# A first route over thirteen batches instead of twelve, one step later, with its stores in pairs

## The chip, the cores and the metric

The kernel runs on one core of a Trainium2 chip. The metric is the device time of one execution in microseconds (us). Before the change three runs gave 716.4, 717.88 and 718.25 us; their median, 717.88, is the time that the change is compared with.

## What is computed

A two-layer block on `x` of 16 batches with 128 rows of width 128, with a context `ctx` of 77 rows a batch. All in float32. Cut to what matters:

```python
x = x + tanh(g_xattn[0]) * xattn0(ctx_1024, layernorm(x), mask, ...)   # 16 heads of 64, keys from ctx and x
x = x + tanh(g_ffn[0])   * ffn0(layernorm(x), ...)                     # 128 -> 512 -> 128, gelu
x = x + tanh(g_xattn[1]) * xattn1(layernorm(x), ctx_1024, ...)         # 16 heads of 8, top 32 of 77 scores
x = x + tanh(g_ffn[1])   * moe(layernorm(x), Wr, br, W1, W2)

def moe(x):                                  # rows = 16 * 128 = 2048, 8 experts of 128 -> 512 -> 128
    route = sigmoid(x @ Wr + br)
    e = argmax(route, axis=1)                # one expert a row
    return max(route) * (gelu(x @ W1[e]) @ W2[e])
```

The change touches only the last line: how rows are sorted by expert before the expert products.

## The kernel before, in words

**Steps and slots.** The sixteen batches go through a software pipeline, written out by hand for each engine in its own program. In step i, batch i is prepared, batch i-1 (`A`) does the first attention, i-2 (`A2`) its end and the first feed-forward net, i-3 (`B`) and i-4 (`C`) the second attention, and i-5 (`E`) its output, the layer norm of the router (`r_z`) and the router's logits. A step has eight slots, and the steps run from 0 to 20. Step 18 still has B = 15, C = 14, E = 13; step 19 has C = 15, E = 14; step 20 has E = 15 alone. VectorE (DVE) finds the top 32 of 77 scores in rounds of MAX8 and MATCH_REPLACE, two heads at a time (`top_first`, `top_second`), GpSimd (POOL) subtracts the maximum (`below_max`) and masks (`keep_top`), and computes inverse roots (`rsqrt`: `b_rs`, `f_rs`, `c_rs`), ScalarE (ACT) does exponentials and copies out of PSUM, TensorE (PE) multiplies and transposes. Each engine executes its own instructions in the order in which they are written and waits on semaphores; nothing else orders them.

**Routing.** `ROUTES` splits the batches in groups that are sorted one after the other. For a group, VectorE adds the bias (`route_biases`), ScalarE does the exponential (`route_exps`), VectorE picks each row's expert (`choose`), TensorE counts rows by expert with matmuls (`count_rows`), and VectorE turns the counts into a place in memory for each row (`row_places`). Then GpSimd stores each batch's rows to their places in `z_sorted`, one indirect DMA a batch (`place_row`, "store" below). `PLACE_AT` says in which step and slot which batches are stored, always at the slot's end. The first group is batches 0 to 11: bias and exponential in step 17 slot 0, choice in slot 1, counting in slot 5, places in slot 7, stores one a slot from step 18 slot 0 to step 19 slot 3. The second is 12 to 14, in step 20; the third is batch 15, behind the steps.

**Tiles.** Rows of one expert are packed in tiles of 128; there are at most 23 (`SORTED`). Of the rows of the first group, `FULL` tiles are sure to be full, whatever the routing: with 12 batches five. Their expert and place come from `map_full`, the others' from `map_rest`, behind the third group. For each tile SP (SyncE's queue) loads the rows (`load_tile`, 129 KB), ScalarE's queue loads the expert's first weights (`load_up`, 256 KB, five buffers, `UPS`), and TensorE does transpose (`turn_z`), up-projection (`tile_up`), down-projection (`tile_down`), in the order `tile_up(n + 1)`, `turn_z(n + 2)`, `tile_down(n)`. SP's loads of the full tiles wait for all stores of the first group:

```python
sp.wait_ge(s["map_ready"], 2)
sp.wait_ge(s["rows_placed"], 16 * ROUTES[0][1])
for n in range(FULL):
    load_tile(n)
sp.wait_ge(s["map_ready"], 4)
sp.wait_ge(s["rows_late"], 16 * (NB - ROUTES[0][1]))
```

`turn_z(0)` stands in step 20 slot 4 on TensorE, ahead of the transpose of batch 15's `r_z` in slot 5.

In the profile's rows, `negmax`, `sw`, `m` and `p` are tiles of the two attentions, `xs` holds x, `rows_out` the last x and `r_z` of each batch, `z_ring` the tiles loaded, `raw` the first weights of the experts, `h_ring` the hidden layer. L730 is any transpose, L1048 `tile_up`, L1058 `tile_down`, L1203 any of ScalarE's, L628 a store, L502 and L504 an inverse root, L515 `below_max`, L522 `keep_top`, L508 `spread_keys`, L533 `add_rows`, L528 the copy of `r_z`, L1557 a normalisation, L1629 `route_biases`, L1639 to L1647 `choose`, L1660 to L1663 `row_places`, L1714 the last of `map_rest`, L897 `project_out`.

## Time and profile before

| | us |
|---|---|
| median of three runs | 717.88 |
| the profiled execution | 717.09 |
| its span | 715.3 |
| TensorE busy | 646.1 (90%) |
| VectorE busy | 572.8 (80%) |
| ScalarE busy | 482.1 (67%) |
| GpSimd busy | 447.6 (63%) |

The profiled execution's time has 1.8 us around its span, and is 0.8 us below the median. Times in rows count from the start of the span. An engine's busy share is a mean over the whole; the last 150 us, from step 17 on, differ from the rest, as batches run out and TensorE idles.

### The profile page before, as it was taken

To read this page: it belongs to the slowest core of one execution; us is meant where nothing else is said; L and a number is where in the kernel's file an instruction comes from. 1 tells how busy PE (TensorE), PEld (TensorE's weight loads), DVE (VectorE), ACT (ScalarE), POOL (GpSimd) and SP (SyncE) were. 2 spreads that over 40 slices of the span, in tenths; PEclk is the share of its full clock that TensorE was granted. 3 is DMA by queue.
4 is the path that set the end of the run, shared out by engine and by line. 5 is a ranking of instruction groups with operands and counts; after the bars stand their busy time and mean duration, and the time that the engine had idled before them with its cause. 6 is when DMAs were issued, how large, how long until landed. Compare 5 with 4: busy or idle time off the path is not lost.

```text
span 715.3 us, 19341 instructions
## 1 busy us (share of the span) xinstructions
PE 646.1 (90%) x5007; PEld 525.3 (73%) x5007; DVE 572.8 (80%) x3758; ACT 482.1 (67%) x1331; POOL 447.6 (63%) x689
## 2 busy tenths in 40 slices
PE   5678999999999999999999999999999867766995
PEld 4546577778787877878787878787878656555895
DVE  3275639898989999999989898989899989985331
ACT  1257578798888797878788887878888834322231
POOL 7465676966757576757675757676675725673354
PEclk9989999999999999999999999999999965555998
DMA  7200059991000000000000000000000000114581
GB/s 212 75 1 1 1 165 302 323 288 45 1 3 1 1 1 0 0 0 0 0 0 0 0 0 0 0 0 0 0 0 3 1 1 1 37 53 133 184 239 46
DMA packets 38537, 37.92 MB, mean 53 GB/s; under 512 B 3633, under 2 KB 34249, under 8 KB 38484
## 3 DMA queue, kind: packets, MB, share of 16 engines
q1 hardware_dynamic: 32986, 27.76, 13.8%
q10 hardware_dynamic: 3994, 6.36, 3.1%
q0 software_dynamic: 1504, 3.17, 1.3%
q8 instruction: 24, 0.39, 0.2%
q14 instruction: 29, 0.24, 0.1%
HBM read 16.28 MB, written 21.45 MB: 53 GB/s over the span
## 4 chain that ended last, share of the span: by engine, by line
PE 48%; DVE 34%; issue 7%; POOL 5%; SPq 3%; ACT 1%; DMA 1%; DVEq 0%; POOLq 0%
DVE sw L1585 13%; DVE m L1579 9%; PE bank L730 8%; PE bank L887 6%; PE bank L829 5%; PE bank L958 5%; PE bank L897 4%; DVE negmax L1532 3%; PE score_banks L859 3%; PE bank L1048 3%; PE bank L839 2%; PE bank L1058 2%; PE bank L817 2%; PE bank L921 2%; PE bank L912 2%
## 5 line engine op out<-in xcount | busy, mean ns | idle before, releaser
L1585 DVE MATCH_REPLACE8 sw<-m,sw 128x77 f32<-128x77 f32 x1024 | 219.8, 222 | 0.1
L1579 DVE MAX8 m<-sw 128x8 f32<-128x77 f32 x1024 | 189.0, 225 | 2.3 <-ACT sw L1203 1.3
L1203 ACT ACTIVATE prob<-score_banks,negmax 128x205 f32<-128x205 f32 x256 | 107.5, 433 | 22.1 <-DVE negmax L1532 22.1
L496 POOL TENSOR_TENSOR prob<-prob,inv 128x820 f32<-128x820 f32 x64 | 99.5, 1554 | 18.6 <-DVE inv L1537 18.6
L515 POOL TENSOR_TENSOR sw<-sw,m 128x616 f32<-128x616 f32 x64 | 78.0, 1218 | 50.0 <-DVEq L1566 49.7
L958 PEld LDWEIGHTS bank<-v,p1T 77*128 77x128 f32 x512 | 72.3, 215 | 15.0 <-DVE c_z L1611 5.2
L958 PE MATMUL bank<-v,p1T 77*128 (+1 forms) x512 | 72.1, 269 | 9.8 <-DVE c_z L1611 4.4
L1585 DVE MATCH_VALUE_LOAD sw<-m,sw 128x8 f32 x1024 | 77.2, 75 | 0.0
L1532 DVE TENSOR_REDUCE negmax<-score_banks 128x2 f32<-128x410 f32 x128 | 68.0, 573 | 2.3 <-PE score_banks L859 2.3
L730 PE MATMUL bank<-ident,prob 128*77 128x128 f32 (+1 forms) x512 | 67.3, 274 | 1.6 <-POOL prob L496 1.4
L839 PE MATMUL bank<-raw,kvT 128*77 128x512 f32 (+1 forms) x128 | 67.2, 607 | 0.0
L1203 ACT ACTIVATE h_ring<-bank 128x256 f32<-128x256 f32 (+1 forms) x87 | 38.5, 443 | 42.2 <-PE bank L1058 20.8
L730 PEld LDWEIGHTS bank<-ident,prob 128*77 128x77 f32 (+1 forms) x512 | 58.6, 146 | 9.4 <-POOL prob L496 5.2
L941 PE MATMUL bank<-second_keys,b_q 128*128 128x308 f32 x128 | 53.1, 499 | 8.9 <-ACT p1T L1203 7.9
L829 PE MATMUL bank<-kvT,raw 128*128 128x205 f32 x256 | 59.4, 355 | 1.2 <-DVE xs L1544 0.6
L522 POOL TENSOR_TENSOR p<-sw 128x308 f32<-128x308 f32 x64 | 47.0, 734 | 18.3 <-ACT sw L1203 18.1
L859 PE MATMUL score_banks<-k_sb,q_sb 64*128 64x205 f32 x512 | 57.9, 344 | 0.0
L887 PE MATMUL bank<-ptc,z_ring 77*64 77x128 f32 x512 | 53.1, 285 | 3.3 <-issue 2.6
L829 PEld LDWEIGHTS bank<-kvT,raw 128*128 128x128 f32 x256 | 42.6, 189 | 15.9 <-issue 14.3
L1203 ACT ACTIVATION_READ_ACCUMULATOR prob<-score_banks,negmax 128x1 f32 x256 | 53.0, 207 | 0.0
L1203 ACT ACTIVATE p1T<-bank 77x512 f32<-77x512 f32 x64 | 37.8, 591 | 19.8 <-PE bank L730 16.5
L1203 ACT ACTIVATE sw<-sw 128x616 f32<-128x616 f32 x64 | 46.9, 732 | 5.7 <-POOL sw L515 5.4
(253 smaller groups left out, 1456.1 us busy)
## 6 DMA issues: line engine op xcount, KB each, us to landing
z_sorted<-no_row SPq DMA_DIRECT2D x1, 17415.0 KB, 65.8
raw<-in_L_ffn_W ACTq DMA_DIRECT2D x23, 256.0 KB
z_ring<-z_sorted SPq DMA_DIRECT2D x23, 129.0 KB
w<-in_L_ffn_W SPq DMA_DIRECT2D x8, 256.0 KB, 4.5
raw<-in_L_xattn_Wkv SPq DMA_DIRECT2D x2, 512.0 KB, 8.8
xs<-in_x SPq DMA_DIRECT2D x1, 960.0 KB, 6.9
cx<-in_ctx SPq DMA_DIRECT2D x1, 577.5 KB
raw<-in_L_xattn_Wq SPq DMA_DIRECT2D x1, 512.0 KB, 8.2
```

The lines of the kernel that those rows point to most:

```text
L496: g.tensor_tensor(p, p, inv[:, 4 * q:4 * q + 4].unsqueeze(2).to_broadcast([128, 4, KV]), ALU.mult).then_inc(s["p_norm"], 1)
L515: g.tensor_tensor(v, v, m8[:, 4 * q:4 * q + 4, 0, 0:1].to_broadcast([128, 4, 2 * NK]), ALU.subtract).then_inc(s["sub_done"], 1)
L730: return nc.tensor.transpose(dst, src, ident[0:rows, 0:rows])
L829: last = mm(dst[:, KV * c:KV * c + KV], wkv_in[:, at:at + 128], kvT[:, :], start=True, stop=True)
L839: mm(dst[0:nr, :], kvT[:, r0:r0 + nr], wkv_in[:, INNER + 512 * j:INNER + 512 * j + 512], start=True, stop=True)\
L859: last = mm(SC[:, u, KV * r:KV * r + KV], q_sb[rows[u], q // 2, 2 * (q % 2) + r, :], k_sb[rows[u], q % 2, r, :], start=False, stop=(r == 1 ...
L887: last = mm(dst[64 * u:64 * u + 64, 128 * c:128 * c + 128], v[:, DH * h:DH * h + DH], p[:, 2 * c + u, :], start=not last_part, stop=last_p ...
L958: last = mm(M[:, c:c + D1 + 1], p1T[:, n, :], v1[:, bass.ds(b, 1), 4 * q + n, :].squeeze(1), start=True, stop=True)
L1203: return nc.scalar.activation(dst, src, f, **kw)
L1532: v.tensor_reduce(negmax[:, 2 * p:2 * p + 2], SC[:, :, KV * (p % 2):KV * (p % 2) + KV], AX_X, ALU.max, negate=True).then_inc(s["max_ready" ...
L1579: v.max(m8[:, h, r, :], sw[:, h, src, :]).then_inc(s[name], 1)
L1585: v.match_replace(sw[:, h, 1, :], m8[:, h, r, :], sw[:, h, src, :], TAKEN)\
```

## The change

The first group has thirteen batches (0 to 12). Batch 12's logits exist only at the end of step 17, so bias, exponential, choice, counting and places move from step 17 to step 18, to the same slots. The stores of the group move to step 19, two in each slot from 0 to 5 and one in slot 6. With thirteen batches six tiles are sure to be full, so `FULL` is 6, and 17 tiles are left to the last map. The weights of the sixth tile have no buffer of their own: ScalarE loads them behind the first gelu, and the loads behind the last map start one gelu later. The second group is batches 13 and 14.

```diff
--- before.py
+++ after.py
@@ -45,9 +45,9 @@
     ROW = 2 * D + 2
     COEF, TOKEN = 2 * D, 2 * D + 1
     NOWHERE = 1 << 20
-    ROUTES = ((0, 12), (12, 15), (15, NB))
+    ROUTES = ((0, 13), (13, 15), (15, NB))
     FULL = -(-(ROUTES[0][1] * S - NE * (S - 1)) // S)
-    assert FULL == UPS and (NB * S - FULL * S + NE * (S - 1)) // S <= SORTED - FULL
+    assert FULL == UPS + 1 and (NB * S - FULL * S + NE * (S - 1)) // S <= SORTED - FULL
     assert S == 128 and D == 128 and DH == 64 and HID == 512 and NK * 4 <= 512
 
     with ExitStack() as ctx:
@@ -287,7 +287,7 @@
 
             return (i, slot - 1) if slot else (i - 1, SLOTS - 1)
 
-        PLACE_AT = {(18 + b // 8, b % 8): (b,) for b in range(ROUTES[0][1])}
+        PLACE_AT = {(19, k): tuple(range(2 * k, min(2 * k + 2, ROUTES[0][1]))) for k in range(7)}
         assert max(PLACE_AT) < (20, 0)
         PLACE_AT[20, 6] = tuple(range(*ROUTES[1]))
 
@@ -1063,7 +1063,7 @@
                 now["at"] = at
                 P, A, A2, B, C, E = (at(n) for n in range(6))
                 for slot in range(SLOTS):
-                    if i == 17 and slot == 5:
+                    if i == 18 and slot == 5:
                         count_rows(0)
                     if i == 20 and slot == 4:
                         count_rows(1)
@@ -1313,7 +1313,7 @@
                     before = slot_before(i, slot) if i is not None else None
                     if UP_AT.get(before, PST) < PST:
                         bias_stage(UP_AT[before])
-                    if i == 17 and slot == 0:
+                    if i == 18 and slot == 0:
                         route_exps(0)
                     if i == 20 and slot == 0:
                         route_exps(1)
@@ -1354,7 +1354,7 @@
                         if E is not None:
                             move(E, c_zT, "cT_psum", "cT_ready")
                         if i == 20:
-                            for n in range(2, FULL):
+                            for n in range(2, UPS):
                                 load_up(n)
                         if A is not None:
                             queries_kept(A, TL, 1, 6)
@@ -1431,6 +1431,8 @@
                 if n >= 2:
                     act.wait_ge(s["ey_psum"], n - 1)
                 fn(hT[:, n % 2, :, :].rearrange("p c q -> p (c q)"), [GZ, TC][n % 2][:, :], ACT.Gelu).then_inc(s["hT_ready"], 1)
+                if n == 0:
+                    load_up(UPS)
                 if n == FULL - 3:
                     act.wait_ge(s["map_ready"], 4)
                     load_up(FULL)
@@ -1739,12 +1741,12 @@
                         v.tensor_tensor(bias_cols[:, :], wu[:, 0, :, D], up_bias, ALU.add).then_inc(s["biases_ready"], 1)
                     if (i, slot) == (20, 0):
                         map_full()
-                    if (i, slot) in ((17, 0), (20, 0)):
-                        route_biases(0 if i == 17 else 1)
-                    if (i, slot) in ((17, 1), (20, 2)):
-                        choose(0 if i == 17 else 1)
-                    if (i, slot) in ((17, 7), (20, 5)):
-                        row_places(0 if i == 17 else 1)
+                    if (i, slot) in ((18, 0), (20, 0)):
+                        route_biases(0 if i == 18 else 1)
+                    if (i, slot) in ((18, 1), (20, 2)):
+                        choose(0 if i == 18 else 1)
+                    if (i, slot) in ((18, 7), (20, 5)):
+                        row_places(0 if i == 18 else 1)
                     if (i, slot) == (20, 5):
                         z_out(0)
                     if i == 1 and 1 <= slot <= 6:
```

GpSimd's instructions from step 18's last slot to the rsqrt of step 19, before (DMA at L628 is a store, the two instructions at its end are `c_rs` of batch 14):

```order
L628 DMA z_sorted<-rows_out,place 17280x258
L515 TENSOR_TENSOR sw<-sw,m 128x616
L628 DMA z_sorted<-rows_out,place 17280x258
L522 TENSOR_TENSOR p<-sw 128x308
L628 DMA z_sorted<-rows_out,place 17280x258
L522 TENSOR_TENSOR p<-sw 128x308
L628 DMA z_sorted<-rows_out,place 17280x258
L515 TENSOR_TENSOR sw<-sw,m 128x616
L628 DMA z_sorted<-rows_out,place 17280x258
L502 TENSOR_SCALAR c_rs<-c_mv 128x1
L504 TENSOR_TENSOR c_rs<-c_rs,half 128x1
```

The same place of the changed kernel:

```order
L533 TENSOR_TENSOR xs<-xs,bo 128x128
L515 TENSOR_TENSOR sw<-sw,m 128x616
L628 DMA z_sorted<-rows_out,place 17280x258 x2
L522 TENSOR_TENSOR p<-sw 128x308
L628 DMA z_sorted<-rows_out,place 17280x258 x2
L522 TENSOR_TENSOR p<-sw 128x308
L628 DMA z_sorted<-rows_out,place 17280x258 x2
L515 TENSOR_TENSOR sw<-sw,m 128x616
L628 DMA z_sorted<-rows_out,place 17280x258 x2
L502 TENSOR_SCALAR c_rs<-c_mv 128x1
L504 TENSOR_TENSOR c_rs<-c_rs,half 128x1
```

Four stores ahead of `c_rs` became eight, in pairs, and the store at the end of step 18 is gone.

VectorE's instructions in step 18 slots 0 and 1, ahead of the normalisation `b_z` of batch 15, before:

```order
L1609 RECIPROCAL c_inv<-bank 128x16
L1611 TENSOR_TENSOR c_z<-bank,c_inv 128x128
L1579 MAX m<-sw 128x8 x2
L1585 MATCH_REPLACE sw<-m,sw 128x77 x2
L1579 MAX m<-sw 128x8 x2
L1585 MATCH_REPLACE sw<-m,sw 128x77 x2
L1557 TENSOR_SCALAR b_z<-xs,b_mv,b_rs 128x128
```

The same place of the changed kernel, whose line numbers are two higher:

```order
L1587 MATCH_REPLACE sw<-m,sw 128x77 x2
L1581 MAX m<-sw 128x8 x2
L1587 MATCH_REPLACE sw<-m,sw 128x77 x2
L1641 TENSOR_SCALAR route<-route 128x104
L1642 RECIPROCAL route<-route 128x104
L1643 TENSOR_REDUCE r_max<-route 128x13
L1644 TENSOR_TENSOR r_eq<-route,r_max 128x104
L1645 TENSOR_TENSOR r_eq<-r_eq,r_pri 128x104
L1646 TENSOR_REDUCE r_top<-r_eq 128x13
L1647 TENSOR_TENSOR chosen<-r_eq,r_top 128x104
L1649 TENSOR_SCALAR rows_out<-r_max,tg 128x13
L1559 TENSOR_SCALAR b_z<-xs,b_mv,b_rs 128x128
```

The eight instructions of `choose` moved in ahead of `b_z`; they stood ahead of `b_z` of batch 14, a step earlier.

ScalarE's first instructions of the tile loop behind the table load, before (a TENSOR_LOAD reads the expert's number, the DMA loads its weights):

```order
L1203 ACTIVATE h_ring<-bank 128x512 x3
L1306 TENSOR_LOAD tile_expert
L1306 ISA x2
L1307 ISA
L1307 DMA raw<-in_L_ffn_W 128x512
L1306 TENSOR_LOAD tile_expert
```

And in the changed kernel:

```order
L1203 ACTIVATE h_ring<-bank 128x512
L1306 TENSOR_LOAD tile_expert
L1306 ISA x2
L1307 ISA
L1307 DMA raw<-in_L_ffn_W 128x512
L1203 ACTIVATE h_ring<-bank 128x512 x3
```

One load moved ahead to stand behind the first gelu, the others stand behind the fourth instead of the third.

## Rows read from the trace of the kernel before

**Rows 1.** The page, part 4: shares of the chain that ended last
```profile
PE 48%; DVE 34%; issue 7%; POOL 5%; SPq 3%; ACT 1%; DMA 1%; DVEq 0%; POOLq 0%
```

**Rows 2.** Timeline around the last map, all engines: start, us, engine, line, op
```profile
666.21 0.17 DVE L1714 TENSOR_SCALAR tile_expert<-t_exp 128x18 int32<-128x18 f32 x1
...
667.14 12.93 SPq L393 DMA_DIRECT2D z_ring<-z_sorted  x11
...
667.73 1.06 PE L1058 MATMUL bank<-w,h_ring 128*128 x8
...
670.62 0.33 PE L730 MATMUL bank<-ident,z_ring 128*128 128x128 f32 x1 [0.94 <-DMA z_ring<-z_sorted]
...
671.52 1.15 PE L1058 MATMUL bank<-w,h_ring 128*128 x8 [0.58 <-issue]
...
675.47 1.06 PE L1058 MATMUL bank<-w,h_ring 128*128 x8
...
677.37 1.06 PE L1058 MATMUL bank<-w,h_ring 128*128 x8
```

**Rows 3.** Timeline of GpSimd, steps 18 and 19
```profile
608.54 1.23 POOL L628 DMA_INDIRECT z_sorted<-rows_out,place  x1 [0.44 <-issue]
...
622.52 1.23 POOL L515 TENSOR_TENSOR sw<-sw,m 128x616 f32<-128x616 f32 x1
...
634.16 1.21 POOL L515 TENSOR_TENSOR sw<-sw,m 128x616 f32<-128x616 f32 x1 [1.26 <-DVEq L1566]
...
641.86 0.99 POOL L628 DMA_INDIRECT z_sorted<-rows_out,place  x1 [0.16 <-DVE c_mv L1553]
642.92 0.19 POOL L502 TENSOR_SCALAR c_rs<-c_mv 128x1 f32<-128x1 f32 x1
```

**Rows 4.** Timeline of GpSimd, stores one behind another
```profile
659.74 0.96 POOL L628 DMA_INDIRECT z_sorted<-rows_out,place  x1 [0.30 <-issue]
```

**Rows 5.** Timelines of step 17: bias add and choice; then `row_places`
```profile
570.52 1.00 DVE L1629 TENSOR_TENSOR route<-route,br 128x96 f32<-128x96 f32 x1
...
573.82 0.45 DVE L1639 TENSOR_SCALAR route<-route 128x96 f32<-128x96 f32 x1
...
576.57 0.34 DVE L1557 TENSOR_SCALAR b_z<-xs,b_mv,b_rs 128x128 f32<-128x128 f32 x1
...
598.78 0.25 DVE L1660 TENSOR_TENSOR place_e<-score_banks,expert_base 128x96 f32<-128x96 f32 x1
...
599.12 2.32 POOL L508 TENSOR_TENSOR second_keys<-k1T,head_mask 128x1232 f32<-128x1232 f32 x1
...
599.64 1.83 DVE L1663 CAST place<-place_f 128x12 uint32<-128x12 f32 x1
```

**Rows 6.** Timelines of VectorE in step 18
```profile
608.85 0.93 DVE L1557 TENSOR_SCALAR b_z<-xs,b_mv,b_rs 128x128 f32<-128x128 f32 x1
...
615.14 0.38 DVE L1579 MAX8 m<-sw 128x8 f32<-128x77 f32 x2 [1.25 <-ACT sw L1203]
...
622.93 0.92 DVE L1557 TENSOR_SCALAR r_z<-rows_out,c_mv,c_rs 128x128 f32<-128x128 f32 x1
```

**Rows 7.** VectorE's wait; two windows, busy of PE, PEld, DVE, ACT, POOL, then clock
```profile
580.97 0.35 DVE L1544 SCALAR_TENSOR_TENSOR xs<-bank,tg,xs 128x128 f32<-128x128 f32 x1 [1.27 <-PE bank L897]
...
572.00:574.00 2.00, 1.10 (x16) 0.89 (x16) 1.97 (x16) 1.89 (x4) 1.26 (x3) 1.00 0.00 0
578.00:580.00 2.00, 2.00 (x11) 2.00 (x11) 1.69 (x15) 0.42 (x1) 0.73 (x1) 0.50 0.00 0
```

**Rows 8.** SP's map read and its wait for the stores, step 20's loads and transpose
```profile
L390 SPq TENSOR_LOAD <-tile_row x23: 129/270/462, 647.0 to 691.7; - x23
...
L396 SPq EVENT_SEMAPHORE  x1: 17/17/17, 644.4 to 644.4; - x1
...
653.00 2.45 ACTq L1307 DMA_DIRECT2D raw<-in_L_ffn_W  x3
...
656.29 0.45 PE L730 MATMUL bank<-ident,r_z 128*128 128x128 f32 x1 [2.09 <-DVE r_z L1557]
```

## The prediction

> **What bounds the kernel now.** I read the page's chain first, then the chain piece by piece over the last 60 us, then the timelines of GpSimd, VectorE and TensorE around steps 17 to 20. The chain is shared by TensorE and VectorE, with GpSimd at 5% [rows 1]. By place it is more telling. Steps 17 and 18 are VectorE's: it runs the top-k rounds of the last batches almost without a pause. From 634 us on, GpSimd carries the end of step 19: `below_max`, one store, `keep_top`, one store, and so on until the rsqrt `c_rs` of batch 14 at 642.92 [rows 3]. After step 20 the expert tiles are TensorE's at one tile in 1.9 us (`tile_down` at 675.47 and at 677.37) [rows 2]. Between these two lies one hole: the last map is ready at 666.39, the first tile behind it is asked for at 667.14, its transpose starts 3.5 us later at 670.62, when the data is there, and the `tile_down` that stands behind that transpose starts at 671.52 [rows 2]. The `tile_down` before it started at 667.73, so that this one was due at 669.6: a hole of 1.9 us.
>
> Three numbers decide: what the sixth full tile gives back there, what the stores cost where they now stand, and how much earlier VectorE reaches step 19.
>
> **The sixth tile.** With six tiles known before the last map, TensorE does one more tile (1.9 us, [rows 2]) before it needs the map. The hole is just as long. The load behind the map lands at 670.6 and would be wanted at 669.6 + 1.9 = 671.5, so it is in time. I take 1.8 us. The bounds are 1.9 and 1.2, the latter if the weights of tile 6, twice a tile's bytes, come 0.7 late: ScalarE now issues the loads of tiles 6 and 7 behind the fourth gelu, not the third, so that they have less time before they are needed. The extra weight load behind the first gelu falls in a quiet stretch: nothing.
>
> **The stores.** A store holds GpSimd for 0.99 us [rows 3], and 0.30 more when one follows another [rows 4], 1.29 in all. The eight stores of step 18 go. There VectorE is what is late, so they give little, priced below. In step 19 there are thirteen for four. Ahead of `c_rs` of batch 14 stand eight now, where four stood. That stretch has no slack: from 634.16 to 642.92 are 8.8 us, and two `below_max` at 1.21 and four stores at 0.99 [rows 3] fill 6.4 of them, two `keep_top` and the gaps between instructions (0.16 ahead of the store at 641.86) the rest. Four more at 1.29 are 5.2 us. Behind `c_rs` hang r_z of batch 14, its logits, and then the contexts of batch 15, its `x`, and r_z of batch 15, whose transpose stands at 656.29 [rows 8]. `keep_top` of batch 15's last quarter now has two more stores before it, too, but TensorE gets to its transposes only behind the logits of batch 14, so that hides. All of it moves by 5.2 us less VectorE's lead.
>
> **VectorE's lead.** GpSimd's run of step 19 begins when VectorE closes the top-k pair at 634.16 [rows 3]. What reaches that place earlier or later:
> - Step 17 loses the bias add, 1.00 us at 570.52 of which 0.1 lies beside the next instruction, and the choice, from 573.82 to 576.57, 2.8 us [rows 5]: 3.7.
> - It has a wait of 1.27 us at 580.97 on `project_out` [rows 7]. With 3.7 us less work VectorE gets there earlier and must not wait longer. `project_out` starts behind b_z, which moves by the same 3.7, but also behind `attend` and a set of contexts. At the half clock, 1.2 of 2.4 GHz (the row of 578 to 580 has 0.50, and TensorE is busy all through it [rows 7]) its sixteen matmuls take some 3.4 us and the wait becomes 1.8; 572 to 574 still had 1.00 [rows 7], TensorE now idles less there, and at the full clock the matmuls need half and the wait is gone. So this is a loss of 0.5 or a gain of 1.2. I take the gain as likelier, at 1.1: the clock fell after a stretch with TensorE about half busy, and the idle time on b_z is what goes.
> - Step 17 also loses `row_places`: 598.78 to 601.47, 2.7 us, of which 1.83 is one cast of 128x12 beside GpSimd's 2.32 us `spread_keys` [rows 5].
> - Step 18 gains the bias add again (0.9: `below_max` runs beside it as before) and the choice (2.8), now ahead of b_z of batch 15. Minus 3.7. The wait of 1.25 us at 615.14 [rows 6] hangs on b_z and stays.
> - b_z took 0.93 us beside the first store, r_z 0.92 beside a `below_max` that a store had made late, where 0.35 is the free duration [rows 3, 5, 6]. Without stores both are free: 1.1 in all.
> - `row_places` in step 18 has no `spread_keys` beside it (there is no batch left for it): 1.1 us for four instructions, with `keep_top` and `add_rows` near, 1.5.
>
> Sum of the lead: 3.7 + 1.1 + 2.7 - 3.7 + 1.1 - 1.5 = 3.4. I take 3.0, since not every free microsecond survives the close waits; the bounds are 1.4 (half clock, cast blocked) and 3.9.
>
> **The first tiles.** SP may load the first tile only when all stores of the first route have landed. Before, the last of them was issued at 641.86 and SP passed at 644.4, 2.5 us later, while the map came only at 647.0 [rows 3, 8]: hidden by 2.6 us. Now the thirteenth store starts 7.2 us after `c_rs` (four more ahead of it at 1.29, the rsqrt, a copy and a `keep_top` at some 2 us together). Landing 2.5, some 0.9 us that SP needs to read the row and issue (from the map at 666.39 to 667.14 it is 0.75 [rows 2]), and 2.5 to 3.5 us until tile 0 is in (3.5 as behind the map, with weight loads beside it [rows 2]; three weight loads go out at 653.00 [rows 8], so they are beside it here too; 2.5 as a guess without them, from the landing of a store) put tile 0 at 13.1 to 14.1 us behind `c_rs`. Its transpose stands in TensorE's queue ahead of that of r_z of batch 15, which started at 656.29, 13.4 behind `c_rs` [rows 3, 8]. So r_z waits behind a tile that isn't there: 0.3 to 1.3 us, I take 1.0. Before, this wait was nothing.
>
> **Sum.** 5.2 - 3.0 + 1.0 - 1.8 = +1.4 us. The profiled execution took 717.09 us with a span of 715.3; with 1.4 it is 718.5. The median of the runs, 717.88, is 0.8 above it, so I forecast 719.3. About 0.3%, 2.2 us, is what a measurement of this kernel can tell from no change, so this is no change that can be told, on the slow side.
>
> **Rivals.**
> - *The clock stays half at `project_out`, lead 1.7.* For it: it was half there. Against it: the idle time ahead of it shrinks. 5.2 - 1.7 + 1.0 - 1.8 = +2.7: 720.6, slower. Chance 0.27.
> - *A store gets ahead of r_z of batch 14.* The row: b_z started 0.31 us into a store and ended with it, 0.93 for 0.35 [rows 3, 6]. In step 19 a store stands right behind `c_rs`, and r_z is released by the same rsqrt. A store starts 0.16 us behind its predecessor [rows 3]; VectorE should be a little quicker. If it loses, r_z comes 0.9 later: 5.2 - 3.0 + 0.9 + 1.0 - 1.8 = +2.3, 720.2; with the small lead it is more. Chance 0.10. The Trainium skill ("SBUF — State Buffer", Who interferes with whom) says that a VectorE tensor_scalar in its two-port mode and a GpSimd instruction exclude each other, and that whichever was issued first holds the ports to its end. By that rule moving stores close to normalisations is a danger, and taking them out of step 18 a gain; the b_z row agrees.
> - *Faster: the lead covers the stores.* If the choice in step 18 lay wholly in waits (VectorE has one of 1.25 us there, behind b_z [rows 6]), and step 17 gave all it holds, the lead would be 3.7 + 1.2 + 2.7 = 7.6 less the 1.5: 6.1, with the port gains 7.2. Then 5.2 - 7.2 + 1.0 - 1.8 = -2.8: 715.1. It decides from a lead of 6.6. Against it: the choice stands ahead of b_z and the wait hangs on b_z, so that they add. Chance 0.10.
> - *A wash.* Lead 3.9 and tile 0 in time: -0.2, 717.7. It is inside "no change". Chance 0.10; my forecast has 0.43, with a range of its own from 718.0 to 720.0.
>
> So: slower 0.37, same 0.53, faster 0.10. Range 716.9 to 722.0: above it the half clock together with a store ahead of r_z (717.88 + 3.6 and a late weight load), below it only the faster case.
>
> **What the profile would show.** Right: `c_rs` of batch 14 one to four us later than 642.92, with eight stores ahead of it in pairs 1.29 us apart; TensorE idle on the load of tile 0 ahead of r_z's transpose; no idle on a z load behind the last map; the cast of `row_places` far under 1.8 us; b_z of batch 15 near 0.35. Wrong: the close at 634.16 earlier by under 1.4 or over 3.9; stores in pairs at another pace than 1.29; the tile loop with a new hole at tile 6 or 7, which would be the weights.

## The result, and the profile after

Seven runs of the changed kernel gave 717.67 to 722.53 us, median 720.17; seven of the kernel before, on the same chip, 716.4 to 718.25, median 717.85. The ratio is 1.0040, with a 95% interval of 1.0023 to 1.0057. So it is slower by about 0.4%, where I forecast 719.3 us and no change that can be told, on the slow side. The median is 0.9 us above my number and inside its range; the interval's lower end lies a little under the 0.3% that I called the least one can tell.

The page of the changed kernel has the span, and in part 4 the chain that ended last by engine:

```profile
span 715.9 us, 19345 instructions
...
PE 47%; DVE 33%; issue 8%; POOL 5%; SPq 3%; DMA 2%; ACT 1%; DVEq 0%; POOLq 0%
```

Against [rows 1] TensorE and VectorE have lost a per cent each; "issue" and "DMA" have won one. This execution, 717.67 us, is the fastest of the seven, so its span must not be set against that of before as it stands. I count from a marker that stands ahead of every instruction that the change touches: the residual with which VectorE ends step 16's work on `xs`. VectorE's timeline has it at 570.25 us before and at 568.90 in this profile:

```profile
570.25 0.35 DVE L1544 SCALAR_TENSOR_TENSOR xs<-bank,tg,xs 128x128 f32<-128x128 f32 x1 [0.26 <-DVE sw L1585]
```

```profile
568.90 0.35 DVE L1546 SCALAR_TENSOR_TENSOR xs<-bank,tg,xs 128x128 f32<-128x128 f32 x1 [0.26 <-DVE sw L1587]
```

From the marker to the end are 145.05 us before (715.3 - 570.25) and 147.0 after (715.9 - 568.90): +1.95 us, and 1.35 us of this execution's good time have nothing to do with the change.

The timeline of all engines shows the new bottleneck, from the top-k pair that begins GpSimd's run of step 19 to batch 15's router transpose:

```profile
628.68 1.22 POOL L515 TENSOR_TENSOR sw<-sw,m 128x616 f32<-128x616 f32 x1 [4.53 <-DVEq L1568]
...
630.08 1.23 POOL L628 DMA_INDIRECT z_sorted<-rows_out,place  x1 [0.18 <-issue]
...
631.61 0.96 POOL L628 DMA_INDIRECT z_sorted<-rows_out,place  x1 [0.30 <-issue]
...
642.70 0.19 POOL L502 TENSOR_SCALAR c_rs<-c_mv 128x1 f32<-128x1 f32 x1
...
643.65 0.35 DVE L1559 TENSOR_SCALAR r_z<-rows_out,c_mv,c_rs 128x128 f32<-128x128 f32 x1 [6.19 <-POOL c_rs L504]
643.73 1.04 POOL L628 DMA_INDIRECT z_sorted<-rows_out,place  x1 [0.19 <-issue]
...
649.59 0.37 ACTq L1307 DMA_DIRECT2D raw<-in_L_ffn_W  x1
649.80 0.97 POOL L628 DMA_INDIRECT z_sorted<-rows_out,place  x1 [0.30 <-issue]
...
652.85 2.45 ACTq L1307 DMA_DIRECT2D raw<-in_L_ffn_W  x3
...
654.46 4.82 SPq L393 DMA_DIRECT2D z_ring<-z_sorted  x5
...
657.87 0.45 PE L730 MATMUL bank<-ident,z_ring 128*128 128x128 f32 x1 [4.13 <-DMA z_ring<-z_sorted]
658.35 0.29 DVE L1723 COPY z_T<-bank 128x128 f32<-128x128 f32 x1 [3.16 <-PE bank L730]
658.56 0.34 DVE L1559 TENSOR_SCALAR r_z<-rows_out,c_mv,c_rs 128x128 f32<-128x128 f32 x1
...
659.05 0.45 PE L730 MATMUL bank<-ident,r_z 128*128 128x128 f32 x1 [0.73 <-DVE r_z L1559]
```

At 628.68 is the `below_max` that stood at 634.16 in [rows 3]: 63.91 us behind the marker before, 59.78 now, so VectorE's lead is 4.13 us. The stores come in pairs, the second 0.30 behind the first, as forecast. `c_rs` of batch 14 starts at 642.70, 73.80 us behind the marker and before (642.92) 72.67: between `below_max` and `c_rs` are 14.02 us where there were 8.76, 5.26 more. Then the last store starts at 649.80, SP loads tile 0 at 654.46, and TensorE, which had been idle for 4.13 us, transposes it at 657.87. Only then, at 659.05, comes the transpose that stood at 656.29 in [rows 8]. The chain of waits names the pieces between:

```profile
649.80 3.65 DMA z_sorted<-rows_out,place
...
653.52 0.47 SPq L390
...
654.46 3.27 DMA z_ring<-z_sorted
```

Store 3.65 us until it has landed, SP 1.0 us to read and issue, load 3.27 us. It is 7.10 us from `c_rs` to the last store and 16.35 to the router transpose; before it was 13.37.

VectorE's timeline answers to [rows 5 to 7]. The wait of 1.27 us on `project_out` is gone, b_z of batch 15 and r_z of batch 13 have their free duration, and so has the cast:

```profile
574.86 0.34 DVE L1546 SCALAR_TENSOR_TENSOR xs<-bank,tg,xs 128x128 f32<-128x128 f32 x1
...
603.64 0.34 DVE L1559 TENSOR_SCALAR b_z<-xs,b_mv,b_rs 128x128 f32<-128x128 f32 x1
...
617.07 0.34 DVE L1559 TENSOR_SCALAR r_z<-rows_out,c_mv,c_rs 128x128 f32<-128x128 f32 x1
...
624.17 0.17 DVE L1665 CAST place<-place_f 128x13 uint32<-128x13 f32 x1
```

At the end of the kernel the hole behind the last map is gone, as TensorE's timeline shows: `tile_down` stands every 1.9 us with no wait on a load, where [rows 2] had 3.8 us between 667.73 and 671.52.

```profile
670.42 1.06 PE L1058 MATMUL bank<-w,h_ring 128*128 x8
...
672.32 1.06 PE L1058 MATMUL bank<-w,h_ring 128*128 x8
```

From the router transpose to the end of the span are 56.85 us; before 59.01 (715.3 - 656.29). So 5.26 - 4.13 + 2.98 - 2.16 = +1.95.

### The profile page after: what moved, and what is told of

It is laid out like the page before. It is cut to its first block, busy times and chain, and to the rows that moved or that the text cites. A ratio compares the mean times of both kernels' runs of the same rounds, so it can differ in the third digit from the quotient of the medians.

```text
span 715.9 us, 19345 instructions
## 1 busy us (share of the span) xinstructions
PE 640.9 (90%) x5009; PEld 521.0 (73%) x5009; DVE 570.1 (80%) x3758; ACT 481.8 (67%) x1331; POOL 447.3 (62%) x689
## 4 chain that ended last, share of the span: by engine, by line
PE 47%; DVE 33%; issue 8%; POOL 5%; SPq 3%; DMA 2%; ACT 1%; DVEq 0%; POOLq 0%
DVE sw L1587 13%; DVE m L1581 9%; PE bank L730 7%; PE bank L887 6%; PE bank L829 5%; PE bank L958 4%; PE bank L897 4%; DVE negmax L1534 3%; PE score_banks L859 3%; PE bank L1048 3%; PE bank L839 2%; PE bank L1058 2%; PE bank L817 2%; PE bank L921 2%; PE bank L912 2%
## 5 line engine op out<-in xcount | busy, mean ns | idle before, releaser
L887 PE MATMUL bank<-ptl,z_ring 128*64 128x128 f32 x512 | 50.0, 272 | 0.0
```

The lines of the kernel that those rows point to most:

```text
L887: last = mm(dst[64 * u:64 * u + 64, 128 * c:128 * c + 128], v[:, DH * h:DH * h + DH], p[:, 2 * c + u, :], start=not last_part, stop=last_p ...
```

## Experiments

All kernels of a group ran beside the kernel before on one chip; ratios are to it, with 95% intervals. Edits are on the changed kernel unless said otherwise.

### late_z: tile 0's transpose behind the router

```diff
@@ TensorE, step 20 slot 4 @@
-                        pe.wait_ge(s["map_ready"], 2)
-                        turn_z(0)
@@ TensorE, behind the steps @@
             reach(pe, "lg_ready", NB - 1, 1)
+            turn_z(0)
             turn_z(1)
@@ VectorE: z_out(0) from step 20 slot 5 to here @@
             route_biases(2)
+            z_out(0)
             choose(2)
```

> The changed kernel, with the transpose of tile 0 and its copy moved from step 20 behind the last step, so that neither TensorE nor VectorE stands on tile 0 ahead of r_z of batch 15. Theory 1 (the wait for tile 0 ahead of r_z is what the late stores cost): TensorE's idle time of 4.1 us there goes, r_z's transpose comes about 13.5 us behind c_rs of batch 14 instead of 16.4, and the time falls by 2.5 to 3 us against the changed kernel, to about 717.5, no different from before. Theory 2 (what is lost is lost in GpSimd's late c_rs, and the wait for tile 0 only moves to the tile loop): less than 0.7 us.

Measured: 719.2 us, ratio 1.0003 [0.9991, 1.0016]. The wait is gone, as TensorE's and GpSimd's timelines say:

```profile
647.60 0.19 POOL L502 TENSOR_SCALAR c_rs<-c_mv 128x1 f32<-128x1 f32 x1
...
661.07 0.45 PE L730 MATMUL bank<-ident,r_z 128*128 128x128 f32 x1 [2.42 <-DVE r_z L1558]
```

From `c_rs` at 647.60 to the router transpose are 13.47 us, as before the change (13.37). That settles where the 2.98 us come from. Part of the cure is paid back, as the loop over tiles now starts later behind that transpose: the first store of output rows stands 12.36 us behind it (673.43), in the changed kernel 11.29 (670.34). How much time is won is less certain. The profile has 147.4 us from the marker to the end, 1.2 less than a profile of the changed kernel at the same clock (148.7, after_again below). The ratio, 1.0003 for 1.0040, says 2.7 us, near the 2.5 to 3 that were expected. The medians, 719.2 for 720.17, can't be set against each other as they stand, because the kernel before, too, ran slower beside this one (718.49 for 717.85).

### early3: three stores moved ahead of step 19

```diff
-        PLACE_AT = {(19, k): tuple(range(2 * k, min(2 * k + 2, ROUTES[0][1]))) for k in range(7)}
+        PLACE_AT, at = {}, 0
+        for when, n in (((18, 7), 3), ((19, 0), 1), ((19, 1), 1), ((19, 2), 1), ((19, 3), 1),
+                        ((19, 4), 2), ((19, 5), 2), ((19, 6), 2)):
+            PLACE_AT[when] = tuple(range(at, at + n))
+            at += n
```

> The changed kernel, with three stores moved ahead into step 18 slot 7, where GpSimd idles 4.5 us after row_places, one a slot in step 19 slots 0 to 3 and two a slot in 4 to 6. Theory 1: four fewer stores ahead of c_rs of batch 14 bring it 5.2 us forward, the last store 3.7 us forward, tile 0 with it, and the time falls by 3.7 us against the changed kernel, to about 716.5. Theory 2 (c_rs then waits for VectorE's and TensorE's work on batch 14, so stores ahead of it cost little): 1 us.

Measured: 715.93 us, ratio 0.9959 [0.9943, 0.9974], faster than both kernels. Timelines of GpSimd and TensorE:

```profile
640.28 0.18 POOL L507 TENSOR_SCALAR c_rs<-c_mv 128x1 f32<-128x1 f32 x1
...
656.11 0.45 PE L735 MATMUL bank<-ident,z_ring 128*128 128x128 f32 x1 [4.50 <-DMA z_ring<-z_sorted]
```

`c_rs` is 68.55 us behind this profile's marker (571.73), 5.25 less than the 73.80 of the changed kernel at the same clock: four stores fewer ahead of it, and the 5.2 us come back whole. The median lies a little under the 716.5 that were expected. The three that went to step 18's end fill time in which GpSimd waits for VectorE anyway. The wait for tile 0 stays.

### five_full: thirteen batches, but only five full tiles

```diff
-    FULL = -(-(ROUTES[0][1] * S - NE * (S - 1)) // S)
+    FULL = UPS
...
-                if n == 0:
-                    load_up(UPS)
```

> The changed kernel, but only five tiles ahead of the last map, as before the change (the map and the weight loads of before). Theory 1: the hole of 1.9 us in TensorE's tile loop is back, and the time rises by 2.1 us against the changed kernel, to about 722.3. Rival: the hole was hidden by the late first tiles, 0.5 us or less.

Measured: 723.31 us, ratio 1.0058 [1.0042, 1.0073]. TensorE's timeline has the hole again:

```profile
677.96 0.33 PE L730 MATMUL bank<-ident,z_ring 128*128 128x128 f32 x1 [1.01 <-DMA z_ring<-z_sorted]
678.80 1.16 PE L1058 MATMUL bank<-w,h_ring 128*128 x8 [0.51 <-issue]
```

From the router transpose to the end are 58.64 us, 1.8 more than the 56.85 of the changed kernel's first profile and 2.3 more than the 56.3 of its second: about the forecast for the sixth tile. From the marker to the end are 150.9 us, 2.2 more than in the second, which has the same clock, for 2.1 expected. The ratio, 1.0058 for 1.0040, says 1.3 us.

### pairs12: the kernel before, with its twelve stores two in a slot of step 19

```diff
-        PLACE_AT = {(18 + b // 8, b % 8): (b,) for b in range(ROUTES[0][1])}
+        PLACE_AT = {(19, k): (2 * k, 2 * k + 1) for k in range(ROUTES[0][1] // 2)}
```

> The kernel before, twelve batches in step 17, with nothing changed but the stores: two in each of slots 0 to 5 of step 19. Theory 1: c_rs of batch 14 5.2 us later, less 1.1 us from normalisations in step 18 that no store holds up, tile 0 late by about 1.5 us, the hole in the tile loop as before: +5.5 us against before, 723.4. Rival: the stores in step 18 held VectorE up by more than the two normalisations, so that taking them out gives back 3 us: +2.5.

Measured: 722.82 us, ratio 1.0055 [1.0037, 1.0072], some 4 us for the 5.5 expected; in the profile it is 5.2 from the marker to the end. VectorE's and TensorE's timelines:

```profile
582.58 0.35 DVE L1544 SCALAR_TENSOR_TENSOR xs<-bank,tg,xs 128x128 f32<-128x128 f32 x1 [1.28 <-PE bank L897]
...
662.29 0.45 PE L730 MATMUL bank<-ident,z_ring 128*128 128x128 f32 x1 [2.66 <-DMA z_ring<-z_sorted]
```

The wait on `project_out` is as before, as nothing in step 17 changed. With no store in step 18 VectorE reaches step 19 at 62.72 us behind the marker for 63.91: 1.19 us, what b_z and r_z lose beside GpSimd (forecast 1.1). `c_rs` is 4.07 us later than before (76.74 for 72.67), and tile 0 is waited for here too, with twelve batches: it comes with the stores' place and doesn't need the larger group.

### late_early: late_z and early3 together

> Theory 1 (two waits add up: the stores of rows stand ahead of c_rs of batch 14, and TensorE's wait for tile 0 stands ahead of batch 15's router transpose, the second being longer the earlier the first is mended): with both edits c_rs(14) comes at 68.6 us behind the marker (the residual of step 16) as in early3, and from there to the router transpose 13.5 us in place of 17.0; the loop over tiles starts 1.1 us later behind that transpose, as in late_z. So 2.4 us less than early3: 713.5, ratio 0.993 to the kernel before. Theory 2 (the tile loop is bound by the last store and the load of tile 0 either way): no gain on early3, 715.9, ratio 0.996.

Measured: 713.46 us, ratio 0.9943 [0.9924, 0.9962], the lowest median of all, as Theory 1 has it. From `c_rs` to the router transpose are 13.45 us, as GpSimd's and TensorE's timelines have it:

```profile
641.05 0.18 POOL L507 TENSOR_SCALAR c_rs<-c_mv 128x1 f32<-128x1 f32 x1
...
654.50 0.45 PE L735 MATMUL bank<-ident,r_z 128*128 128x128 f32 x1 [2.13 <-DVE r_z L1563]
```

`c_rs` is 70.70 us behind the marker, not the 68.6 of early3, since this profile has the half clock at `project_out` (see after_again): 2.15 us later.

### keep_clock: no idle time of TensorE ahead of `project_out`

```diff
+                        if i == 17:
+                            reach(pe, "exp_done", NB - 1, SLOTS)
+                            for n in range(8):
+                                turn(S0[:, 0:128], ident[:, :])
                         if C is not None:
                             contexts(C, 0, 4)
```

The eight transposes write a bank that nobody reads any more.

> Eight transposes of the identity fill TensorE's idle 0.9 us in slot 1 of step 17, ahead of the contexts of batch 14. Theory 1 (in some executions of one and the same kernel the granted clock falls at this place, so that project_out of batch 15 takes 3.6 us in place of 2.0 and VectorE waits 2.1 us for it; with the hole filled it never falls there): the profile shows project_out at 2.0 us and no wait of VectorE behind it, its spread of times is smaller than the changed kernel's (717.67 to 722.53), and its median about 1 us lower, 719.2, ratio 1.0025. Theory 2 (what sets the clock is the long stretch of the steps before, not this hole): the profile shows either, and the median stays at 720.2, or up to 0.5 above for the transposes that delay the contexts.

The reason for this one: in the profiles of late_z and five_full `project_out` of batch 15 took 3.62 us, not the 2.0 of the changed kernel's first profile, though nothing ahead of it differs. Measured: 720.13 us in twelve runs, 719.04 to 721.50, ratio 1.0036 [1.0025, 1.0048]. TensorE's timeline, and the windows with clock (columns as in [rows 7]):

```profile
573.15 1.09 PE L730 MATMUL score_banks<-ident 128*128 128x128 f32 x8
...
575.17 2.00 PE L897 MATMUL bank<-raw,h_ring 128*128 128x128 f32 x16
...
572.00:574.00 2.00, 2.00 (x26) 1.71 (x24) 1.68 (x12) 1.99 (x4) 1.76 (x4) 1.00 0.04 8
574.00:576.00 2.00, 2.00 (x19) 1.90 (x18) 2.00 (x18) 0.90 (x3) 0.49 (x1) 1.00 0.00 0
```

The profile is what Theory 1 says, and from the marker on it takes as long as the changed kernel's first (147.0 us), so that the added transposes cost nothing there. The median isn't: it stays at 720.1, where 719.2 was expected. The spread of 2.5 us shows nothing either way. It is half of the 4.9 of the changed kernel's first seven runs, but its second seven, beside these on the same chip, spread over 1.7 us around 720.56. What the filled hole does to the median stays open.

### after_again: the changed kernel a second time

> The changed kernel once more. Theory 1 (two clocks in step 17): its times spread over 4 us as before (717.7 to 722.5), median 720.2, ratio 1.003; its profile shows project_out of batch 15 either at 2.0 us with no wait of VectorE, or at 3.6 us with a wait of 2.1 us, and the span behind the marker of step 16 is 147.0 us in the one case and 149 in the other. Theory 2 (the first profile's time of 717.67 owes to something else): project_out at 2.0 us again and a span that differs elsewhere.

Measured: 720.56 us in seven runs, 720.15 to 721.87, ratio 1.0043 [1.0028, 1.0058]. Timelines of TensorE and VectorE, and windows:

```profile
575.68 3.62 PE L897 MATMUL bank<-raw,h_ring 128*128 128x128 f32 x16
...
579.34 0.35 DVE L1546 SCALAR_TENSOR_TENSOR xs<-bank,tg,xs 128x128 f32<-128x128 f32 x1 [2.08 <-PE bank L897]
...
572.00:574.00 2.00, 1.08 (x18) 0.87 (x14) 1.81 (x16) 1.84 (x4) 1.74 (x4) 0.90 0.00 0
574.00:576.00 2.00, 2.00 (x11) 2.00 (x11) 2.00 (x18) 0.08 (x1) 0.09 (x1) 0.50 0.03 8
...
578.00:580.00 2.00, 2.00 (x12) 2.00 (x11) 0.52 (x2) 0.24 (x1) 0.00 (x0) 0.50 0.00 0
```

The same instructions, another clock: 2.4 GHz granted until 572, 0.90 of it in the window to 574, then 1.2 GHz (0.50) to 580. `project_out` takes 3.62 us and VectorE waits 2.08 for it. In the first profile all of these windows have 1.00 and `project_out` took 2.01. From the marker to the end are 148.67 us (719.9 - 571.23), 1.67 more; expected were 2. So two executions of one kernel differ at this place as Theory 1 says. What it said of the times did not come: they spread over 1.7 us, not over 4.

### w1_late and w1_behind: weight loads out of the stores' way

ScalarE's queue loads the first weights of five experts at 649.59 and 652.85, beside the last store and the load of tile 0. Both of these variants issue the first two in slot 4 of step 20. w1_late issues the other three in slot 6, w1_behind behind the exponential of the third group:

```diff
@@ ScalarE, both: step 20 slot 0 @@
-                        act.wait_ge(s["map_ready"], 2)
-                        for n in range(2):
-                            load_up(n)
@@ ScalarE, both: step 20 slot 4 @@
                         if i == 20:
-                            for n in range(2, UPS):
+                            act.wait_ge(s["map_ready"], 2)
+                            for n in range(2):
                                 load_up(n)
@@ w1_late @@
                     if slot == 6:
+                        if i == 20:
+                            for n in range(2, UPS):
+                                load_up(n)
@@ w1_behind @@
             route_exps(2)
+            for n in range(2, UPS):
+                load_up(n)
```

> The five loads of up weights are issued 3 to 10 us later (two in slot 4 and three in slot 6 of step 20), so that none runs beside the last store of rows of the first route. Theory 1 (the store's 3.65 us to landing, against the 2.5 of my forecast, come from the weight loads beside it): it lands in 2.5 us, tile 0 arrives 1.1 us sooner or more, and so does batch 15's router transpose: 719.0 to the changed kernel's 720.2, ratio 1.0015. Theory 2 (3.65 us is what an indirect store takes to land in any case): the store and the wait stay, 720.2 or above where a tile then waits for its weights.

Measured: 721.04 us, ratio 1.0050 [1.0033, 1.0067], not the 719.0 of Theory 1. The chain of waits, then ScalarE's queue and its next copy:

```profile
652.40 2.46 DMA z_sorted<-rows_out,place
...
655.88 2.03 DMA z_ring<-z_sorted
...
660.39 2.73 ACTq L1307 DMA_DIRECT2D raw<-in_L_ffn_W  x3
...
663.17 0.18 ACT L1203 ACTIVATE route<-bank 128x8 f32<-128x8 f32 x1 [3.18 <-issue]
```

The store landed in 2.46 us instead of 3.65 and tile 0 in 2.03 instead of 3.27; from `c_rs` (645.30) to the router transpose (659.23) are 13.93 us. Only the store's landing is a clean test, as nothing of the weights is issued beside it now. The first two weight loads go out at 655.99, right behind the load of tile 0, so that its shorter time isn't that of a load alone. The gain is lost behind it: issuing three loads holds ScalarE for 2.73 us, and the copy of batch 15's logits, for which TensorE waits, stands behind them. Hence w1_behind, which keeps them behind that copy.

> The changed kernel with its loads of up weights out of the way of the stores, and this time of ScalarE's copies too: two in slot 4 of step 20, three behind the exponential of the third route. Theory 1 (the weight loads stretch the landing of the last store and the load of tile 0 by 2.4 us together, and w1_late lost that again because ScalarE's three issues stood ahead of the logits of batch 15): from c_rs of batch 14 to batch 15's router transpose 13.9 us as in w1_late (16.35 in the changed kernel), and from there to the first store of output rows 11.3 us as in the changed kernel (13.7 in w1_late): 718.0, ratio 1.000 to the kernel before. Theory 2 (the loop over tiles is bound by the weights wherever they stand): the second stretch stays above 13 us, and the time at 720 to 721.

Measured: 718.49 us, ratio 1.0018 [1.0001, 1.0035]. Chain, then timelines of GpSimd and TensorE:

```profile
650.86 2.47 DMA z_sorted<-rows_out,place
...
643.77 0.19 POOL L502 TENSOR_SCALAR c_rs<-c_mv 128x1 f32<-128x1 f32 x1
...
657.03 0.45 PE L730 MATMUL bank<-ident,z_ring 128*128 128x128 f32 x1 [2.22 <-DMA z_ring<-z_sorted]
658.21 0.45 PE L730 MATMUL bank<-ident,r_z 128*128 128x128 f32 x1 [0.73 <-DVE r_z L1559]
```

14.44 us to the router transpose, and 10.94 from there to the first store of output rows (669.15): 25.4 together, for the 25.2 of Theory 1 and the 27.6 of the changed kernel. From the marker to the end are 144.9 us, 2.1 less than in the changed kernel's first profile, which has the same clock. The median is 1.7 us below 720.17, but the twelve runs lie between 716.6 and 722.0 and the interval overlaps that of the changed kernel, so that the times alone don't decide it.

### late_early_w1: the three together

> All three: earlier stores, turn_z(0) behind the logits, weights behind the stores. In late_early the first tile was still loaded late: its last store landed 3.93 us after it began, and the chain runs through it. Theory 1: the store lands in 2.5 us, tile 0 comes 1.5 to 2 us sooner, and the loop over tiles starts up to 1 us sooner (its other feed, the chain of z_T and weights of tile 0, sets the limit): 712.5, ratio 0.9925. Theory 2 (tile loop bound by the instructions behind the router transpose, not by tile 0): no gain on late_early, 713.5, ratio 0.994.

Measured: 714.02 us, ratio 0.9952 [0.9935, 0.9970]. The 712.5 of Theory 1 did not come. In the profile the last store landed in 2.71 us and the stretch from router transpose to the end is 58.14 us for late_early's 59.2, as Theory 1 says; in the times there is no gain on late_early's 713.46, as Theory 2 says. The intervals overlap: this one is not decided.

### before_late_z: late_z's edit on the kernel before

> The kernel before with turn_z(0) and its copy moved behind batch 15's logits, as in late_z. There tile 0 was in time, so nothing is won. Theory 1 (the wait for tile 0 is new with the change): batch 15's router transpose no sooner than before by over 0.5 us, and the loop over tiles starts about 1 us later as in late_z: 718.6, ratio 1.001. Theory 2 (the old order cost time before too): faster by 1 us or more, ratio 0.998 or less.

Measured: 718.78 us, ratio 1.0013 [1.0000, 1.0027]. GpSimd's and TensorE's timelines:

```profile
642.53 0.19 POOL L502 TENSOR_SCALAR c_rs<-c_mv 128x1 f32<-128x1 f32 x1
...
655.91 0.45 PE L730 MATMUL bank<-ident,r_z 128*128 128x128 f32 x1 [2.41 <-DVE r_z L1556]
```

13.38 us, as before (13.37): there was no wait to take away. The stretch behind it, to the end, is 0.7 us longer (59.7 for 59.0), which is the price of the new order where tile 0 is in time. The control bears out that the wait is the change's own.

## Why the forecast was right or wrong, point by point

The profiles side by side, in us. The "pair" is the `below_max` at which GpSimd's run of step 19 begins; "router" is batch 15's router transpose. Where stores stand ahead of the pair's place it says nothing of VectorE.

| kernel | marker | `project_out` | marker to pair | marker to `c_rs` | `c_rs` to router | router to end | marker to end |
|---|---|---|---|---|---|---|---|
| before | 570.25 | 3.63 | 63.91 | 72.67 | 13.37 | 59.0 | 145.1 |
| before_late_z | 569.87 | 3.64 | 63.90 | 72.66 | 13.38 | 59.7 | 145.7 |
| pairs12 | 571.86 | 3.64 | 62.72 | 76.74 | 14.87 | 58.6 | 150.2 |
| changed, 1st | 568.90 | 2.01 | 59.78 | 73.80 | 16.35 | 56.8 | 147.0 |
| changed, 2nd | 571.23 | 3.62 | 61.93 | 75.91 | 16.42 | 56.3 | 148.7 |
| keep_clock | 571.63 | 2.00 | 59.77 | 73.79 | 16.33 | 56.8 | 147.0 |
| five_full | 571.84 | 3.62 | 61.94 | 75.93 | 16.29 | 58.6 | 150.9 |
| late_z | 571.66 | 3.62 | 61.93 | 75.94 | 13.47 | 58.0 | 147.4 |
| w1_late | 571.51 | 2.00 | 59.78 | 73.79 | 13.93 | 59.9 | 147.6 |
| w1_behind | 570.01 | 2.01 | 59.77 | 73.76 | 14.44 | 56.7 | 144.9 |
| early3 | 571.73 | 2.01 | - | 68.55 | 17.01 | 56.9 | 142.5 |
| late_early | 570.35 | 3.62 | - | 70.70 | 13.45 | 59.2 | 143.4 |
| late_early_w1 | 570.07 | 3.38 | - | 69.74 | 13.45 | 58.1 | 141.3 |

Each row is one execution. On what an edit is worth, the last column (set against a row with the same `project_out`) and the ratios differ by up to 2.4 us. The sizes of the gains are known no better than that.

- **The stores, +5.2: right.** 5.26 measured, and early3 gives 5.25 back.
- **VectorE's lead, 3.0: right on the mean by luck, and the mean is of two things.** The pair stands at 59.77 to 59.78 or at 61.93 to 61.94: a lead of 4.13 or of 1.98 us. (late_early_w1, where the clock changed within `project_out`, lies between: its `c_rs` at 69.74 us, for 68.55 in early3 and 70.70 in late_early.) I had taken one outcome and rounded it down, and that this meets the mean of the two, 3.05, is luck. The 4.13 is over the 3.9 that I gave as the bound and as a sign of being wrong. It follows `project_out`, which runs at either clock. The step put this as a question with one answer, "a loss of 0.5 or a gain of 1.2", and took the gain; the rival at half clock had a lead of 1.7 and 720.6 us. Both happen, in executions of one kernel, and both were sized too low by little: the sum of the terms was 3.4, and the difference between the two is 2.15, not 1.7. Why the larger lead is 0.7 above my sum shows at VectorE's next residual on `xs`, which ends step 17 (605.96 before, 597.49 after): up to there 7.1 us are won for 7.5 in the sum, and from there to the pair 2.99 are lost, where the terms add up to 4.1 (3.7 and 1.5, less 1.1). The terms that can be seen alone: b_z and r_z 1.17 (0.93 and 0.92 to 0.34 each) for 1.1, and 1.19 by pairs12; the cast 1.83 to 0.17 beside nothing.
- **The wait for tile 0, +1.0: the step that failed, by size.** 2.98 measured, and late_z shows that it is this wait. Two terms were too low. "Landing 2.5" came from a store with nothing beside it; here it was 3.65, and 2.46 and 2.47 once the weight loads were moved. I had put them beside the load of tile 0 but not beside the store. And I let r_z wait only for TensorE's transpose of the tile, whereas VectorE's copy of the transposed tile stands ahead of r_z itself: in the profile transpose 657.87, copy 658.35, r_z 658.56, its transpose 659.05. That is 1.18 us behind the tile's, where I had counted some 0.6. With the weights out of the store's way the stretch is 13.93 and 14.44 us. That the second is what I had written for it (13.4 + 1.0) is chance: the load of tile 0 was shorter there than I had it (2.55 us), and the copy is still ahead of r_z.
- **The sixth tile, -1.8: right.** 2.16 in the profile, 1.8 to 2.3 by five_full, and no hole at tile 6 or 7 for weights. Some 0.4 of the 2.16 is not the tile's: pairs12 and five_full, which have the hole and the late tile 0, take 58.6 us from router to end where the kernel before takes 59.0.
- **Sum.** With the mean of the two leads, 5.26 - 3.05 + 2.98 - 2.16 = +3.0 us. The medians say +2.3 and +3.0. I had +1.4. What is missing in my sum is the wait for tile 0, 2 us, less 0.4 of the sixth tile.
- **The rivals.** The half clock was no rival but the other half of the truth. That its 720.6 us lie nearer to the median (720.17) than my 719.3 is no merit of it, as it has the wait for tile 0 at 1.0, too: at the half clock the whole is 3.6 us (148.67 for 145.05), not 2.7. A store ahead of r_z of batch 14 did not come about: r_z started at 643.65, 0.08 us ahead of the store, and took 0.35. By the rule of the Trainium skill ("SBUF — State Buffer", Who interferes with whom), whoever is issued first holds the ports to its end; the row agrees, since r_z has its free duration. Faster or a wash would have needed tile 0 in time, or nearly: the -0.2 of the wash holds 0.3 for that wait, and with the wait at nothing the sum is -0.5.
- **Landing times.** The Trainium skill ("DMA: Bandwidth & Descriptors", Latency and other measured facts) says that memory answers more slowly under load and that a DMA's fixed cost shrinks when load is light. The three landing times here, 2.46 and 2.47 without and 3.65 us with weight loads beside the store, agree in direction. Whether it is the memory or the DMA engines that the weight loads keep busy, no run here separates. I had the row but not the load.

## What to carry to other kernels

An optional look-ahead (here the transpose of the first tile) that stands in a queue ahead of required work is harmless only as long as its data is early; when a change makes the data later, follow every engine on which part of it stands ahead, not one. Four instructions moved ahead of a critical one in a full stretch cost their whole issue time, and the cure is to put them where that engine waits for another one: the thirteen batches are worth 0.6% (0.4 to 0.8) by the times when three stores go to step 18's end and tile 0 behind the router. Read a DMA's landing time together with what runs beside it in the row, and ask what will run beside it after the change.

## What the runs showed of the hardware

- The same instructions with the same activity around them ran at two clocks. Of the nine profiles with the changed step 17 and no added transposes, four have the full clock, 2.4 GHz, through `project_out` (2.00 to 2.01 us), and five have 1.2 GHz granted for most or all of it (3.38 to 3.62 us). In after_again TensorE was busy for 1.08 us of the window 572 to 574 and the clock fell in it; in w1_late it was busy for 1.09 us of the same window and the clock stayed. What decides between them is not in the rows. With the idle time filled (keep_clock) the one profile has the full clock, which is too few to say that it always has. The window of w1_late:

```profile
572.00:574.00 2.00, 1.09 (x17) 0.86 (x17) 1.80 (x12) 1.99 (x4) 1.75 (x4) 1.00 0.00 0
```

- The marker, which lies ahead of all edits, stands between 568.90 and 571.86 us in these profiles. This spread of almost 3 us has nothing to do with the steady steps. An earlier residual on `xs` on VectorE stands at 161.78 us in the changed kernel's first profile and at 164.84 in five_full's, and from there to the marker all thirteen profiles take 407.0 to 407.1 us. The spread is made at the start of the kernel, and it sits in every median here. The two timelines:

```profile
161.78 0.35 DVE L1546 SCALAR_TENSOR_TENSOR xs<-bank,tg,xs 128x128 f32<-128x128 f32 x1 [0.55 <-PE bank L921]
```

```profile
164.84 0.35 DVE L1544 SCALAR_TENSOR_TENSOR xs<-bank,tg,xs 128x128 f32<-128x128 f32 x1 [0.55 <-PE bank L921]
```

- An indirect store of 128 rows holds GpSimd for 0.95 to 1.05 us (1.23 the first of the kernel) and the next starts 0.30 later, beside weight loads or not. It is its landing that the loads stretch: 2.46 and 2.47 us without them, 3.34 to 3.93 in the profiles with two weight loads issued beside the last store.
- Issuing three direct loads of 256 KB held ScalarE for 2.45 us in the changed kernel and for 2.73 in w1_late, where other work stood behind them: a queue's issues are not free for the engine that makes them.
